# Second layer's attention on f16 high and low parts turned by transposing DMAs, with norms on ScalarE

## The chip, the cores and the metric

One core of a Trainium2 chip runs the whole kernel. The metric is the device time of one execution in microseconds (us); lower is better. TensorE (PE) multiplies and can also transpose, VectorE (DVE) and ScalarE (ACT) do elementwise work and reach PSUM, GpSimd (POOL) does elementwise work on SBUF only, and SyncE (SP) issues the DMAs. Each engine runs its own list of instructions strictly in order and meets the others at semaphores.

## The reference, cut to what matters

Two layers work on x, 32 sequences of 64 tokens of 256 numbers. The first is an eight-head cross attention and a mixture of eight experts. The second layer, where the change lies, is

```
xn   = layernorm(x)                                   # norm 3
s    = xn @ ctx^T / sqrt(256), masked keys -> -1e30   # per sequence, 64 x 64
x    = x + tanh(g_xattn[1]) * softmax(s) @ ctx
xn   = layernorm(x)                                   # norm 4
x    = x + tanh(g_ffn[1]) * FFN2(xn)                  # four experts by token position, silu(gate)*up, down
```

## The kernel before, in words

All engines run the same loop of half steps. There are 39 steps n of 8 half steps i, and h = 8n + i numbers a half step. Up to h = 255 each half step does one head of the first attention; from h = 26 on, each pair of half steps also does one unit of the feed-forward network: 24 matmuls for the gate into psG (even h), 24 for the up half into psU (odd h), tanh and the cast of the high part on ACT (`unit_tanh`, `unit_high`), two multiplications on DVE (`gate_mul`, `up_mul`), the low f16 part on POOL (`h_low`, L583), the down matmuls (`unit_down`) in the two half steps after that, and `add_expert` on DVE. In this way each f32 product is made from f16 parts, high and low. The 128 units of the first layer are followed by eight units of the second, two for each of four groups k. Their gate matmuls stand at h = 282, 284, 286, 288, 292, 294, 300 and 302. `late_y_out` (ACT), `late_y_turn` (PE) and `late_out` (DVE) bring a finished group back to token order, and `store_out` stores it.

The second attention runs in eight rounds t of four sequences each, woven into the half steps from h = 262 on. `late_base(t)` = 264 + 4t, and `late_at` gives each engine the steps r = h - late_base(t) from -2 to 7, so that two rounds are in flight. In round t:

- r = -2: DVE takes the statistics (`late_stats`, after the last `add_expert` of these tokens) and the mask (`late_masks`); POOL does the norm (`late_norm`: a power, L597, and two 128x256 subtract-and-multiply instructions, L601).
- r = 0 and 1: PE turns the normed x into psT and the context into ps1 (f32 transposes, L1007), ACT copies both (L762).
- r = 2: PE makes the scores in f32 into psV, DVE masks them (`late_masked`, L1361), ACT takes the exponentials (`late_exps`, L767).
- r = 3: PE turns them (L1100), ACT copies. r = 4: PE multiplies with the context in f32 (`late_read`), DVE adds to x (`late_attend`) and takes the statistics of norm 4; POOL does norm 4.
- r = 6 and 7: PE turns the result into psM, ACT and DVE cut it into the f16 parts of x4T.

In addition, four half steps (h = 267, 271, 275, 279) cut the second layer's weights into parts: `late_w_high` on ACT and `late_w_low` on DVE (L1335, two instructions).

The first attention's probabilities already go through transposing DMAs: `turn(g)` on SP moves a 128x1024 f16 tile, high and low part, from p_parts to p_turn (L428). SP's list is in order too: an issue waits for the semaphores of the issue ahead of it.

Of the kernel before, what the change touches and what calls it, by code (L numbers as in the profile page):

```python
# [62 lines left out]
Y_OUT_AT = [8 * TAIL_STEP + at for at in (26, 33, 37, 44)]  # L63
Y_TURN_AT = [8 * TAIL_STEP + at for at in (32, 36, 38, 45)]
# [5 lines left out]
X_SCALE = 256.0  # L70
G_UNSCALE = 1.0 / (W_SCALE * X_SCALE)
# [16 lines left out]
def build(nc, A, out):  # L88
# [14 lines left out]
    with ctx:  # L103
# [41 lines left out]
            d0_loaded d1_loaded dw_hi dw_split xt3_done ctxT_done sc_done sc_masked  # L145
            c_exp pT_ready pT_done read_done xn4T xn4_hi xn4_split cx0_loaded cx1_loaded
            d_yevac d_yT d_out xn3_ready xn4_ready xn3T cxT ln3_in ln4_in out0_stored out1_stored
# [60 lines left out]
        ctxT = lb("ctxT", [P, 2, KT, P], F32)  # L208
        x3T = lb("x3T", [P, 2, KT, P], F32)
        xn3 = lb("xn3", [P, 2, D], F32)  # L210
        d_gu = lb("d_gu", [P, 2, NE1, KT, 2 * NI1], F16)
        d_dn = lb("d_dn", [P, 2, NE1, IB1, D], F16)
        d_st = lb("d_st", [P, 2, 1536], F32)
        x4T = lb("x4T", [P, 4, 2, KT, NE1, P], F16)
        xn4 = lb("xn4", [P, 2, D], F32)
        neg = lb("neg", [P, 2, P], F32)
        pc = lb("pc", [P, 2, P], F32)
        pT = lb("pT", [P, 2, P], F32)
        cstat = lb("cstat", [P, 2, 2, 6], F32)
        cmv = lb("cmv", [P, 2, 2, 2], F32)  # L220
        cve = lb("cve", [P, 2, 2], F32)
        crs = lb("crs", [P, 2, 2], F32)
        low = lb("low", [P, 2], F32)
        csum = lb("csum", [P, 2], F32)
# [44 lines left out]
        def late_y_banks(k):  # L269


            return (psT[:, :], ps1[:, :, :].rearrange("p a b -> p (a b)")) if k % 2 == 0 else (psV[:, :], psM[:, :])
# [53 lines left out]
        def late_cut_at(n, i):  # L326


            e = (8 * (n - TAIL_STEP) + i) // 4
            return e if i % 4 == 3 and 0 <= e < NE1 else None  # L330
# [31 lines left out]
        def _(sp):  # L362
# [38 lines left out]
            def load_late_ctx(j):  # L401
                if j >= 2:
                    sp.wait_ge(s["read_done"], j - 1)
                sp.dma_start(ctx2[:, j % 2, :, :], A["ctx_2048"].rearrange("(j u b) s d -> j (b s) u d", u=2, b=2)[j]
                             ).then_inc(s[f"cx{j % 2}_loaded"], 16)

            def open_late():
# [5 lines left out]
                             ).then_inc(s["mask_m_loaded"], 16)  # L413

# [17 lines left out]
            def step(n):  # L432
                q, par = n // 2, n // 2 % 2
                even = n % 2 == 0
                for i in range(8):
# [19 lines left out]
                    for t, r in late_at(n, i):  # L455
                        if r == 5 and t + 2 < ROUNDS:
                            load_late_ctx(t + 2)
                    out_group = group_at(Y_TURN_AT, g - 1)
# [5 lines left out]
                if n == TAIL_STEP - 2:  # L464
# [3 lines left out]
                if n == TAIL_STEP - 1:  # L468
                    for e in range(2):
                        load_late_weights(e)  # L470
# [31 lines left out]
        def _(pool):  # L502
# [91 lines left out]
            def late_norm(t, kind):  # L594

                pool.wait_ge(s[f"ln{3 + kind}_in"], t + 1)
                st.link(pool.tensor_tensor(crs[:, kind, :], cve[:, kind, :], minus_half[:, 0:2], ALU.pow))  # L597
# [15 lines left out]
            def step(n):  # L613
                q, tail = n // 2, tail_pair(n)
                for i in range(8):
# [31 lines left out]
        def _(act):  # L647
# [112 lines left out]
            def late_copy(sem_in, j, dst, ps, sem_out):  # L760
                act.wait_ge(s[sem_in], j + 1)
                act.activation(dst, ps, ACT.Copy).then_inc(s[sem_out], 1)  # L762

            def late_exps(t):
                act.wait_ge(s["sc_masked"], t + 1)
                for u in range(2):
                    act.activation(pc[:, u, :], psV[:, u * P:u * P + P], ACT.Exp, bias=low[:, u:u + 1], scale=-1.0,  # L767
                                   accum_out=csum[:, u:u + 1]).then_inc(s["c_exp"], 1)

            def late_x_high(t):  # L770

                act.wait_ge(s["xn4T"], t + 1)
                for u in range(2):
                    at = t % 2 * 64 + 32 * u
                    act.activation(x4T[:, t // 2, 0, :, :, at:at + 32],
                                   psM[:, u * D:u * D + D].rearrange("p (k q e) -> p k e q", k=KT, e=NE1),
                                   ACT.Copy, scale=X_SCALE).then_inc(s["xn4_hi"], 1)

# [16 lines left out]
            def step(n):  # L795
                q, tail = n // 2, tail_pair(n)
                for i in range(8):
# [19 lines left out]
                    for t, r in late_at(n, i):  # L817
                        if r == 0:
                            late_copy("xn3T", t, x3T[:, :, :, :].rearrange("p u k t -> p (u k t)"), psT[:, :], "xt3_done")
                        elif r == 1:  # L820
                            late_copy("cxT", t, ctxT[:, :, :, :].rearrange("p u k t -> p (u k t)"),
                                      ps1[:, :, :].rearrange("p a b -> p (a b)"), "ctxT_done")
                        elif r == 2:
                            late_exps(t)
                        elif r == 3:
                            late_copy("pT_ready", t, pT[:, :, :].rearrange("p u t -> p (u t)"), ps1[:, 0, :], "pT_done")
                        elif r == 6:
                            late_x_high(t)
                    e = late_cut_at(n, i)
# [18 lines left out]
        def _(pe):  # L848
# [154 lines left out]
            def late_turn(bank, src, done):  # L1003
                for u in range(2):
                    for k in range(KT):
                        at = (u * KT + k) * P
                        last = pe.transpose(bank[:, at:at + P], src[:, u, k * P:k * P + P], ident[:, :])  # L1007
                last.then_inc(s[done], 1)

            def late_unit_in(u, bank, which, done):  # L1010
# [3 lines left out]
                for e in range(NE1):  # L1014
                    j = 0
                    for kt in range(KT):
                        for wp, xp in ((0, 0), (1, 0), (0, 1)):
                            last = mm(bank[:, e * P:e * P + P], d_gu[:, wp, e, kt, i0:i0 + P], x4T[:, k, xp, kt, e, :],
# [4 lines left out]
            def late_unit_gate(u):  # L1023
# [4 lines left out]
                if u % 2 == 0:  # L1028
                    pe.wait_ge(s["xn4_split"], 8 * (k + 1))
# [23 lines left out]
            def late_y_turn(k):  # L1053

                pe.wait_ge(s["d_yevac"], 2 * k + 2)
                if k == 0:
                    pe.wait_ge(s["xt3_done"], ROUNDS)
                    pe.wait_ge(s["pT_done"], ROUNDS)
                elif k == 1:
                    pe.wait_ge(s["x3_done"], NPAIR)  # L1060
                    pe.wait_ge(s["xn4_split"], 4 * ROUNDS)
                else:
                    pe.wait_ge(s["d_out"], 2 * (k - 1))
                for tt, bank in enumerate(late_y_banks(k)):
# [7 lines left out]
            def late_read(t, r):  # L1072
# [413 lines left out]
```

## Time and profile before

| | |
|---|---|
| median of 3 runs | 871.92 us (870.4 to 872.4) |
| the profiled execution's own time | 872.53 us |
| its span, first to last instruction | 870.8 us |
| busy in the span: PE, DVE, POOL, ACT | 779.9, 674.5, 625.2, 595.7 us |
| mean granted TensorE clock | 0.960 of full |

The span is what the trace shows; the own time is 1.73 us more. Busy times are sums over stages that differ: up to 700 us PE is busy nearly all the time, after that no engine is.

### The profile page before, as it was taken

Reading aid. Unit: us, or ns where it says so; the run is one execution under the profiler, and the core shown is the slowest. Engines: PE = TensorE matmul, PEld = TensorE weight load, DVE = VectorE, ACT = ScalarE, POOL = GpSimd, SP = SyncE. Lnnn points to the kernel's source line nnn. Section 1 sums busy time; section 2 is a strip of 40 time slices with the busy share of each in tenths; the row PEclk is TensorE's granted clock in tenths of the full one; section 3 lists DMA queues with packets and bytes.
Section 4 is the critical chain, followed back from the end, with each engine's and each line's share of the span. In section 5 each row is a group of like instructions: output and inputs, shape, how many; then the busy total and the mean of one; then the engine's idle time right before and its main releaser. Section 6 shows DMA issues by size and latency. Waiting matters only on the chain. (4 is left out here: it accounts for less than half of the span.)

```text
span 870.8 us, 30114 instructions
## 1 busy us (share of the span) xinstructions
PE 779.9 (90%) x11511; PEld 723.5 (83%) x11511; DVE 674.5 (77%) x2353; ACT 595.7 (68%) x1298; POOL 625.2 (72%) x649
## 2 busy tenths in 40 slices
PE   3466689999999999999999999999999998778876
PEld 2344489999999999999999999999999988667766
DVE  3675778888888888888888888888888865867653
ACT  3366868778787877878787778787877843434432
POOL 4265638787979797888888887979796753666651
PEclk9856789999999999999999999999999999999999
DMA  7579998879899888878899888797889662210002
GB/s 231 165 164 234 243 217 200 142 140 155 145 160 148 147 162 148 162 140 170 142 163 150 161 150 161 142 153 154 141 157 149 112 115 75 72 39 14 26 26 73
DMA packets 319541, 123.00 MB, mean 141 GB/s; under 512 B 274716, under 2 KB 312612, under 8 KB 319396
## 3 DMA queue, kind: packets, MB, share of 16 engines
q1 hardware_dynamic: 318656, 120.53, 72.1%
q8 instruction: 91, 1.49, 0.7%
q10 hardware_dynamic: 740, 0.54, 0.2%
q14 instruction: 54, 0.44, 0.2%
HBM read 45.53 MB, written 8.39 MB: 62 GB/s over the span
## 5 line engine op out<-in xcount | busy, mean ns | idle before, releaser
L591 POOL TENSOR_TENSOR p_parts<-p,p_parts 128x512 f16<-128x512 f32 x256 | 296.6, 1159 | 114.9 <-ACT p_parts L710 104.9
L583 POOL TENSOR_TENSOR hp_lo<-th_ga_h,hp_hi 128x512 f16<-128x512 f32 x136 | 157.7, 1160 | 56.1 <-ACT hp_hi L732 52.8
L850 PE MATMUL psG<-xT,w_gu 128*128 128x128 f16 x3072 | 193.5, 220 | 3.0 <-DVE th_ga_h L1286 2.6
L850 PE MATMUL psU<-xT,w_gu 128*128 128x128 f16 x3072 | 194.0, 220 | 0.1
L850 PE MATMUL psY<-w_dn,hp_hi 128*128 128x256 f16 x1024 | 182.2, 273 | 4.5 <-POOL hp_lo L583 4.5
L850 PEld LDWEIGHTS psG<-xT,w_gu 128*128 128x128 f16 x3072 | 176.3, 98 | 7.4 <-DVE th_ga_h L1286 4.9
L850 PEld LDWEIGHTS psU<-xT,w_gu 128*128 128x128 f16 x3072 | 177.7, 98 | 1.0 <-DVE th_ga_h L1294 0.2
L710 ACT ACTIVATE p_parts<-p 128x512 f16<-128x512 f32 x256 | 160.6, 627 | 6.8 <-DMA p_turn<-p_parts 6.3
L1210 DVE CUSTOM_DVE_ANT_0 ps<-ps,mask_in 128x256 f32<-128x256 f32 x256 | 104.2, 448 | 55.3 <-PE ps L850 54.3
L850 PE MATMUL psY<-w_dn,hp_lo 128*128 128x256 f16 x512 | 139.9, 273 | 0.0
L702 ACT ACTIVATE p<-ps,exp_bias 128x256 f32<-128x256 f32 x256 | 107.1, 469 | 47.1 <-DVE exp_bias L1214 46.1
L702 ACT ACTIVATE p<-psT,exp_bias 128x256 f32<-128x256 f32 x256 | 107.3, 473 | 40.2 <-DVE exp_bias L1214 32.7
L726 ACT ACTIVATE th_ga_h<-psG 128x512 f32<-128x512 f32 x136 | 81.2, 597 | 67.8 <-PE psG L850 66.2
L1210 DVE CUSTOM_DVE_ANT_0 psT<-psT,mask_in 128x256 f32<-128x256 f32 x256 | 103.6, 446 | 14.9 <-PE psT L850 14.9
L850 PEld LDWEIGHTS psV<-v_parts,p_turn 128*128 128x128 f16 x2048 | 88.9, 97 | 31.2 <-DMA p_turn<-p_parts 24.7
L850 PEld LDWEIGHTS psY<-w_dn,hp_hi 128*128 128x128 f16 x1024 | 98.3, 98 | 18.8 <-POOL hp_lo L583 6.4
L850 PE MATMUL psV<-v_parts,p_turn 128*128 128x25 bf16 x2048 | 91.4, 175 | 18.7 <-DMA p_turn<-p_parts 16.5
L1286 DVE SCALAR_TENSOR_TENSOR th_ga_h<-th_ga_h,psG 128x512 f32<-128x512 f32 x136 | 93.4, 687 | 12.1 <-ACT th_ga_h L726 11.4
L1294 DVE SCALAR_TENSOR_TENSOR th_ga_h<-psU,th_ga_h 128x512 f32<-128x512 f32 x136 | 92.0, 676 | 4.9 <-PE psU L850 3.7
L732 ACT ACTIVATE hp_hi<-th_ga_h 128x512 f16<-128x512 f32 x136 | 85.8, 631 | 2.0 <-DVE th_ga_h L1294 2.0
L1210 DVE DVE_READ_ACCUMULATOR2_ANT low_max<- 128x1 f32 x512 | 72.6, 142 | 0.0
L1304 DVE SCALAR_TENSOR_TENSOR x_res<-psY,tokw,x_res 128x256 f32<-128x256 f32 x128 | 60.8, 475 | 2.7 <-PE psY L850 2.6
(180 smaller groups left out, 1077.5 us busy)
## 6 DMA issues: line engine op xcount, KB each, us to landing
mask_in<-in_mask_Bx2048x_ff SPq DMA_DIRECT2D x32, 256.0 KB, 3.1
part_scratch<-parts SPq DMA_DIRECT2D x16, 384.0 KB, 3.8
q_stack<-part_scratch SPq DMA_DIRECT2D x62, 96.0 KB
k_stack<-part_scratch SPq DMA_DIRECT2D x62, 96.0 KB
stage<-in_L_ffn_gate_w SPq DMA_DIRECT2D x8, 512.0 KB, 4.9
stage<-in_L_ffn_up_w SPq DMA_DIRECT2D x8, 512.0 KB, 4.9
stage<-in_L_ffn_down_w SPq DMA_DIRECT2D x8, 512.0 KB, 4.3
p_turn<-p_parts SPq DMA_TRANSPOSE x256, 3.6
```

What stands on the lines that cost most here:

```text
L583: pool.tensor_tensor(hp_lo[:, u % 2, :], hb32[:, u % 2, :], hp_hi[:, u % 2, :], ALU.subtract).then_inc(s["h_split"], 1)
L591: pool.tensor_tensor(p_parts[:, g % 4, 1, :, :], p32[:, g % 2, :, :], p_parts[:, g % 4, 0, :, :], ALU.subtract).then_inc(s["plo_done"], 1)
L702: act.activation(p32[:, g % 2, nt, :], score_bank(g)[:, nt, :], ACT.Exp, bias=exp_bias[:, g % 2, nt:nt + 1], scale=-1.0).then_inc(s["exp_d ...
L710: act.activation(p_parts[:, g % 4, 0, :, :], p32[:, g % 2, :, :], ACT.Copy).then_inc(s["phi_done"], 1)
L726: act.activation(th, psG[:, :], ACT.Tanh, scale=0.5 * G_UNSCALE).then_inc(s["tanh_done"], 1)
L732: act.activation(hp_hi[:, u % 2, :], hb32[:, u % 2, :], ACT.Copy).then_inc(s["h_hi"], 1)
L850: return pe.matmul(out_, lhsT, rhs, start=start, stop=stop, skip_group_check=shares_bank)
L1210: dve.tensor_tensor_reduce(out=score_bank(g)[:, nt, :], in0=score_bank(g)[:, nt, :], in1=mask_in[:, n % 2, nt, :], scale=-1.0, scalar=HIGH ...
L1286: dve.scalar_tensor_tensor(out=ga, in0=th, scalar=1.0, in1=psG[:, :], op0=ALU.add, op1=ALU.mult).then_inc(s["gate_used"], 1)
L1294: dve.scalar_tensor_tensor(out=hb32[:, u % 2, :], in0=psU[:, :], scalar=0.5 * G_UNSCALE * G_UNSCALE, in1=ga, op0=ALU.mult, op1=ALU.mult).t ...
L1304: dve.scalar_tensor_tensor(out=x_res[:, row, :], in0=psY[:, y_bank(u), 0:D], scalar=tokw[:, row * NE + e:row * NE + e + 1], in1=x_res[:, r ...
```

## The change

The second attention gets the same treatment as the first: operands are cut into high and low f16 parts on ACT and POOL, turned by DMA, and multiplied in three f16 matmuls where there was one of f32. The f32 transposes on PE and the copies out of PSUM go.

- A round has r = -2 to 10 and `late_base(t)` = 260 + 4t, so that three rounds are in flight and round 0 starts four half steps earlier.
- The norm is done on ACT (`late_norm`, two 128x256 instructions and a 128x512 cast to the high part). POOL keeps the power, one small multiplication (`late_pow`), and takes the low parts (`late_low`, `late_ctx_low`, `late_p_low`).
- SP issues four transposing DMAs a round: the normed x and the context at r = 1, the exponentials at r = 5, norm 4's output at r = 10.
- The scores stand at r = 3 in ps1, the second product at r = 7, `late_attend` and the statistics of norm 4 at r = 8.
- Output groups are turned in psT and psM only, at other half steps; the weights' loads and cuts move by one or two half steps.

In the diff below, "..." marks what is left out: semaphore names, buffer declarations (cx_parts has three buffers, cxT, x3T and pc_parts one), and lines that only rename.

```diff
-Y_OUT_AT = [8 * TAIL_STEP + at for at in (26, 33, 37, 44)]
-Y_TURN_AT = [8 * TAIL_STEP + at for at in (32, 36, 38, 45)]
+Y_OUT_AT = [8 * TAIL_STEP + at for at in (26, 30, 36, 44)]
+Y_TURN_AT = [8 * TAIL_STEP + at for at in (27, 31, 37, 45)]
...
-            return 8 * TAIL_STEP + 4 * t
+            return 8 * TAIL_STEP - 4 + 4 * t
...
-            return [(t, r) for t, r in at if -2 <= r <= 7]
+            return [(t, r) for t, r in at if -2 <= r <= 10]
...
+            def turn_xn3(t):
+                sp.wait_ge(s["xn3_lo"], t + 1)
+                if t:
+                    sp.wait_ge(s["sc_done"], t)
+                turn_late(x3T[:, :, :, :, :].rearrange("p a u k t -> p (a u k) t"),
+                          xn3_parts[:, :, :, :].rearrange("p a u d -> p (a u d)"), "xn3_turned")
+
+            def turn_ctx(t):
+                sp.wait_ge(s["cx_lo"], t + 1)
...
+            def turn_pc(t):
+                sp.wait_ge(s["pl_lo"], t + 1)
+                if t:
+                    sp.wait_ge(s["read_done"], t)
...
+            def turn_xn4(t):
+                sp.wait_ge(s["xn4_lo"], t + 1)
...
                     for t, r in late_at(n, i):
-                        if r == 5 and t + 2 < ROUNDS:
+                        if r == 0 and t + 2 < ROUNDS:
                             load_late_ctx(t + 2)
+                        elif r == 1:
+                            turn_xn3(t)
+                            turn_ctx(t)
+                        elif r == 5:
+                            turn_pc(t)
+                        elif r == 10:
+                            turn_xn4(t)
...
+            def late_pow(t, kind):
...
                 st.link(pool.tensor_tensor(crs[:, kind, :], cve[:, kind, :], minus_half[:, 0:2], ALU.pow))
-                if t:
-                    pool.wait_ge(s[f"xn{3 + kind}T"], t)
-                for u in range(2):
-                    pool.tensor_scalar((xn3, xn4)[kind][:, u, :], x_res[:, 2 * t + u, :], cmv[:, kind, u, 0:1],
-                                       crs[:, kind, u:u + 1], ALU.subtract, ALU.mult).then_inc(s[f"xn{3 + kind}_ready"], 1)
+                pool.tensor_tensor(csh[:, kind, :], cnm[:, kind, :], crs[:, kind, :], ALU.mult
+                                   ).then_inc(s[f"pow{3 + kind}_done"], 1)
+
+            def late_low(t, kind):
+
+                pool.wait_ge(s[f"xn{3 + kind}_hi"], t + 1)
+                parts_of, full = (xn3_parts, xn4_parts)[kind], (xn3, xn4)[kind]
+                pool.tensor_tensor(parts_of[:, 1, :, :], full[:, :, :], parts_of[:, 0, :, :], ALU.subtract
+                                   ).then_inc(s[f"xn{3 + kind}_lo"], 1)
...
                     for t, r in late_at(n, i):
-                        if r == 4:
-                            late_norm(t, 1)
                         if r == -2:
-                            late_norm(t, 0)
+                            late_pow(t, 0)
+                        elif r == -1:
+                            late_ctx_low(t)
+                        elif r == 0:
+                            late_low(t, 0)
+                        elif r == 5:
+                            late_p_low(t)
+                        elif r == 8:
+                            late_pow(t, 1)
+                        elif r == 10:
+                            late_low(t, 1)
...
+            def late_norm(t, kind):
+                act.wait_ge(s[f"pow{3 + kind}_done"], t + 1)
+                if t:
+                    act.wait_ge(s[f"xn{3 + kind}_lo"], t)
+                    act.wait_ge(s[f"xn{3 + kind}_turned"], 16 * t)
...
+                    act.activation(full[:, u, :], x_res[:, 2 * t + u, :], ACT.Identity,
+                                   scale=crs[:, kind, u:u + 1], bias=csh[:, kind, u:u + 1]
...
-                        if r == 0:
-                            late_copy("xn3T", ...
...
+                        if r == -2:
+                            late_ctx_high(t)
+                        elif r == -1:
+                            late_norm(t, 0)
+                        elif r == 4:
                             late_exps(t)
...
+                        elif r == 9:
+                            late_norm(t, 1)
...
+            def late_scores(t):
+
+                pe.wait_ge(s["xn3_turned"], 16 * (t + 1))
+                pe.wait_ge(s["cx_turned"], 16 * (t + 1))
...
+                    for k in range(KT):
+                        for xp, cp in ((0, 0), (1, 0), (0, 1)):
+                            last = mm(ps1[:, 0, u * P:u * P + P], x3T[:, xp, u, k, :], cxT[:, cp, u, k, :],
...
+            def late_read(t):
+
+                pe.wait_ge(s["pl_turned"], 16 * (t + 1))
...
-                        late_read(t, r)
+                        if r == 3:
+                            late_scores(t)
+                        elif r == 7:
+                            late_read(t)
...
+                st.link(dve.tensor_scalar(cnm[:, kind, :], cmv[:, kind, :, 0], -1.0, None, ALU.mult))
...
-                last.then_inc(s["sc_masked"], 1)
+                    st.link(dve.tensor_tensor_reduce(out=at, in0=at, in1=neg[:, u, :], scale=-D ** -0.5 / (X_SCALE * C_SCALE),
...
+                dve.tensor_scalar(low_bias[:, t % 2, :], low[:, t % 2, :], LOG_P_SCALE, None, ALU.add
+                                  ).then_inc(s["sc_masked"], 1)
...
                         if r == -2:
                             late_stats(t, 0)
+                        elif r == 1:
                             late_masks(t)
-                        elif r == 2:
+                        elif r == 3:
                             late_masked(t)
-                        elif r == 4:
+                        elif r == 8:
                             late_attend(t)
                             late_stats(t, 1)
-                        elif r == 7:
-                            late_x_low(t)
```

## Rows read from the trace of the kernel before

**Rows 1.** Busy time by round: stretch, length, five engines, granted clock, DMA share, GB/s

```profile
core 0: us, PE busy (x) PEld busy (x) DVE busy (x) ACT busy (x) POOL busy (x), PEclk, DMA share, GB/s
722.81:738.70 15.89, 13.61 (x164) 12.37 (x162) 7.10 (x21) 5.51 (x14) 6.32 (x7) 0.89 0.06 21
...
767.30:782.90 15.60, 12.12 (x149) 10.61 (x147) 11.52 (x32) 6.74 (x15) 10.24 (x9) 1.00 0.06 18
...
798.49:811.54 13.05, 12.08 (x148) 10.71 (x147) 9.15 (x30) 5.29 (x13) 8.65 (x9) 1.00 0.08 23
...
837.91:852.15 14.24, 9.53 (x101) 8.34 (x99) 7.89 (x26) 4.81 (x13) 5.43 (x5) 0.91 0.11 38
852.15:870.80 18.65, 11.77 (x170) 10.99 (x168) 6.26 (x10) 4.88 (x8) 2.31 (x2) 0.96 0.26 86
```

**Rows 2.** Waits after 700 us: who waited for whom, total us, times, longest

```profile
POOL crs L597 <- DVE cve L1346: 43.3, 16, 5.6
...
PEld psM L1007 <- POOL xn L601: 11.2, 8, 2.8
```

**Rows 3.** Timeline of a round: start, us, engine, line, operation, count [idle before <-releaser]

```profile
811.05 0.66 PE L1007 MATMUL psM<-ident,xn 128*128 128x128 f32 x4 [0.25 <-POOL xn L601]
...
811.54 1.06 PE L850 MATMUL psV<-ctxT,x3T 128*128 128x128 f32 x8
...
820.79 0.72 POOL L597 TENSOR_TENSOR crs<-cve,minus_half 128x2 f32<-128x2 f32 x1 [1.61 <-DVE cve L1346]
...
821.62 2.43 POOL L601 TENSOR_SCALAR xn<-x_res,cmv,crs 128x256 f32<-128x256 f32 x2
```

**Rows 4.** Timeline, VectorE's work around the masking and the second product

```profile
803.34 0.68 DVE L1294 SCALAR_TENSOR_TENSOR th_ga_h<-psU,th_ga_h 128x512 f32<-128x512 f32 x1
...
805.23 0.88 DVE L1374 SCALAR_TENSOR_TENSOR x_res<-psV,cr,x_res 128x256 f32<-128x256 f32 x2 [0.29 <-PE psV L850]
...
806.14 0.89 DVE L1343 BATCH_NORM_STATS2 cstat<-x_res 128x6 f32<-128x256 f32 x2
...
807.50 0.17 DVE L1346 TENSOR_SCALAR cve<-cmv 128x2 f32<-128x2 f32 x1
...
812.64 0.30 DVE L1361 CUSTOM_DVE_ANT_0 psV<-psV,neg 128x128 f32<-128x128 f32 x1 [2.65 <-PE psV L850]
...
812.85 0.14 DVE L1361 DVE_READ_ACCUMULATOR2_ANT low<- 128x1 f32 x1
```

**Rows 5.** Groups and single instructions on POOL: subtractions and small multiplications

```profile
L583 POOL TENSOR_TENSOR hp_lo<-th_ga_h,hp_hi 128x512 f16<-128x512 f32 x136 | 157.7, 1160 | 56.1 <-ACT hp_hi L732 52.8
...
58.33 0.22 POOL L571 TENSOR_TENSOR shift<-mean_var,rstd 128x14 f32<-128x14 f32 x1
...
59.99 0.69 POOL L528 TENSOR_TENSOR rem<-rem,v_parts 128x256 f32<-128x256 f32 x1
...
72.88 0.41 POOL L609 TENSOR_TENSOR on<-o_sum,o_rec 128x128 f32<-128x128 f32 x1 [1.50 <-DMA p_turn<-p_parts]
```

**Rows 6.** SP: instructions on p_turn and on d_st, ns min/median/max, and landing

```profile
L428 SPq DMA_TRANSPOSE p_turn<-p_parts x256: 1231/1267/2821, 42.0 to 710.7; - x128
...
DMA to landing us min/median/max: 3.0/3.6/7.8
...
L417 SPq DMA_DIRECT2D out<-d_st x8: 372/372/1085, 845.7 to 868.0; - x8
...
L1395 DVE TENSOR_TENSOR d_st<-psT,x_res x2: 683/683/683, 845.0 to 858.9; 128x512 f32<-128x512 f32 x2
```

**Rows 7.** Timeline, the cut of one expert's low weight parts on VectorE

```profile
772.56 1.23 DVE L1335 SCALAR_TENSOR_TENSOR d_gu<-d_st,d_gu 128x1024 f16<-128x1024 f32 x1 [0.34 <-ACT d_dn L783]
...
773.70 0.68 DVE L1335 SCALAR_TENSOR_TENSOR d_dn<-d_st,d_dn 128x512 f16<-128x512 f32 x1
```

**Rows 8.** Timeline, an up half of a unit on PE at h = 263

```profile
723.23 1.50 PE L850 MATMUL psU<-xT,w_gu 128*128 128x128 f16 x24
```

**Rows 9.** Group of the first layer's second norm on ScalarE: total us, mean ns

```profile
L747 ACT ACTIVATE xn<-x_res,shift,rstd 128x256 f32<-128x256 f32 x16 | 9.6, 600 | 11.7 <-POOL shift L578 11.6
```

More of the change, by code:

```diff
@@ L70 @@
 X_SCALE = 256.0
+C_SCALE = 16.0
 G_UNSCALE = 1.0 / (W_SCALE * X_SCALE)
@@ L207, in build @@
         m_u8 = lb("m_u8", [P, NPAIR, P], U8)
-        ctxT = lb("ctxT", [P, 2, KT, P], F32)
-        x3T = lb("x3T", [P, 2, KT, P], F32)
+        cx_parts = lb("cx_parts", [P, 3, 2, 2, D], F16)
+        cxT = lb("cxT", [P, 2, 2, KT, P], F16)
+        x3T = lb("x3T", [P, 2, 2, KT, P], F16)
         xn3 = lb("xn3", [P, 2, D], F32)
+        xn3_parts = lb("xn3_parts", [P, 2, 2, D], F16)
+        neg = lb("neg", [P, 2, P], F32)
+        xn4 = lb("xn4", [P, 2, D], F32)
+        xn4_parts = lb("xn4_parts", [P, 2, 2, D], F16)
+        pc = lb("pc", [P, 2, P], F32)
+        pc_parts = lb("pc_parts", [P, 2, 2, P], F16)
+        pT = lb("pT", [P, 2, 2, P], F16)
         d_gu = lb("d_gu", [P, 2, NE1, KT, 2 * NI1], F16)
@@ L324, in late_weight, with late_cut_at @@
                     (d_st[:, e % 2, 1024:1536].rearrange("p (t i) -> p t i", t=IB1), d_dn[:, part, e, :, :]))
-        def late_cut_at(n, i):
+        def late_cut_at(n, i, cut):
             e = (8 * (n - TAIL_STEP) + i) // 4
-            return e if i % 4 == 3 and 0 <= e < NE1 else None
+            return e if i % 4 == cut and 0 <= e < NE1 else None
         def load_stacks(eng, par, q, piece):
@@ L764, in late_exps @@
             def late_exps(t):
                 act.wait_ge(s["sc_masked"], t + 1)
+                if t:
+                    act.wait_ge(s["pl_lo"], t)
+                    act.wait_ge(s["pl_turned"], 16 * t)
                 for u in range(2):
[L767 to L777, printed above, removed]
+                    act.activation(pc[:, u, :], ps1[:, 0, u * P:u * P + P], ACT.Exp, bias=low_bias[:, t % 2, u:u + 1],
+                                   scale=-1.0, accum_out=csum[:, t % 2, u:u + 1]).then_inc(s["c_exp"], 1)
@@ L779, in late_w_high @@
+                act.wait_ge(s["c_exp"], 2 * t + 2)
+                act.activation(pc_parts[:, 0, :, :], pc[:, :, :], ACT.Copy).then_inc(s["pl_hi"], 1)
             def late_w_high(e):
@@ new lines, in late_scores @@
+            def late_scores(t):
+                pe.wait_ge(s["xn3_turned"], 16 * (t + 1))
+                pe.wait_ge(s["cx_turned"], 16 * (t + 1))
+                if t == 0:
+                    pe.wait_ge(s["exp_done"], 2 * 8 * B)
+                else:
+                    pe.wait_ge(s["c_exp"], 2 * t)
+                for u in range(2):
+                    j = 0
+                    for k in range(KT):
+                        for xp, cp in ((0, 0), (1, 0), (0, 1)):
+                            last = mm(ps1[:, 0, u * P:u * P + P], x3T[:, xp, u, k, :], cxT[:, cp, u, k, :],
+                                      start=(j == 0), stop=(j == 5))
+                            j += 1
+                last.then_inc(s["sc_done"], 1)
@@ new lines, in late_read @@
+            def late_read(t):
+                pe.wait_ge(s["pl_turned"], 16 * (t + 1))
+                if t == 0:
+                    pe.wait_ge(s["pv_evac"], B)
+                else:
+                    pe.wait_ge(s["x3_done"], 2 * t)
+                for u in range(2):
+                    for j, (pp, cp) in enumerate(((0, 0), (1, 0), (0, 1))):
+                        last = mm(psV[:, u * D:u * D + D], pT[:, pp, u, :], cx_parts[:, t % 3, cp, u, :],
+                                  start=(j == 0), stop=(j == 2))
+                last.then_inc(s["read_done"], 1)
@@ L1310, in _ @@
             st.link(dve.tensor_scalar(bias_v[:, :], bias_v[:, :], gates[:, 0:1], None, ALU.mult))
+            st.link(dve.tensor_scalar(gates[:, 1:2], gates[:, 1:2], 1.0 / C_SCALE, None, ALU.mult))
             dve.wait_ge(s["qk_copied"], 2)
```

177 lines of the change are left out of this document (72 added, 105 removed).

## The prediction

> **What bounds the kernel now.** Read the page first: its slices show PE busy all through the first attention and the feed-forward units, and only from about 700 us on no engine full. The change touches that last part alone, so everything below is about it. Next, the busy times by round of the second attention [rows 1]: the stretches are cut where the scores of successive rounds start. A round takes 15.6 us while the second layer's weights are cut and 13.05 us later, and in 13.05 us PE is busy 12.1, DVE 9.2, POOL 8.7 and ACT 5.3: nobody is full, so a chain through several engines sets the round. The waits say which [rows 2]: POOL waits 43.3 us, 16 times, for the variance that DVE hands it before each norm, and PE waits for POOL's normed x. One round shows the same in order of time [rows 3]: the power starts at 820.79, the normed x is there at 821.62 + 2.43 = 824.05, and PE, which met the previous norm in the same way at 811.05, goes on to the scores. Two such norms of 0.83 + 2.43 us lie in every round, with DVE's statistics ahead and a PE turn behind.
>
> **What goes.** On POOL 2 x 2.43 us a round. On PE twelve f32 transposes of x and context (0.66 for four [rows 3]), two of exponentials, f32 scores of 1.06 us and a second product of about as much; 24 f16 matmuls of 128 columns take 1.50 us [rows 8], so the twelve of the new scores 0.75, and the six of 256 columns of the new second product the same. PE's 12.1 us fall to about 9. ACT loses four copies and gains nine instructions a round that I bound by 0.60 each [rows 9]: at most 5.3 + 5.4 = 10.7 us. None of the engines' sums fills a round of 13 us. So the next question is which chain closes on itself.
>
> **The chain that I find.** Four half steps hold parts of three rounds. Put S at the end of the scores of round t-1, and go on in the order of the lists.
>
> 1. DVE: `late_masked` of t-1. An instruction starts 0.21 before its accumulator read, which takes 0.14 [rows 4]; with a link behind each now, 0.43 twice, then the new small addition 0.17. S + 1.07.
> 2. DVE: `up_mul`, `add_expert`, `late_attend` of t-2. From 803.34 to 806.14 these take 2.80 us, of which 0.29 waiting [rows 4]. S + 3.58.
> 3. DVE: statistics of norm 4 of t-2, 806.14 to 807.67, plus one more linked small instruction, 0.21. S + 5.35.
> 4. POOL: the power, 0.83 to the next start [rows 3], and the small multiplication, 0.22 [rows 5], with 0.1 of hand-over: S + 6.5. Then, queued behind it, `late_low` of t (1.16), `h_low` of the unit (1.16), `late_p_low` of t-1. This last is 128x256: between 0.41 (half as large) and 1.16 (twice as large), and I take 0.69, the row of that size [rows 5]. S + 9.5.
> 5. SP, which has waited for that low part: `turn_pc` of t-1, and only behind it `turn_xn3` and `turn_ctx` of t. A transposing DMA of 128x1024 holds SP for at least 1.23 us and lands 3.0 at best and 3.6 in the median after its issue [rows 6]. `turn_pc` has half the size: between 0.37, a plain store, and 1.23; I take 0.9, since a transposing issue is the nearer row. The context is issued at S + 9.5 + 0.9 + 1.23 = S + 11.65 and lands, at 3.3, at S + 14.95.
> 6. PE: scores of t, 0.75 and 0.1 of start. S + 15.8.
>
> The scores of t are what DVE masks next, so a round takes 15.8 us. With the shortest values (0.41 for the low part, 0.37 and 3.0) it is 14.7, with the longest (1.16 for the low part, 1.23, 3.6) 16.9. The four rounds in which `late_w_low` follows the masking get 1.14 + 0.6 = 1.74 us more, from start to start [rows 7]: 17.5. PE, ACT and the norms of t+1 lie beside the chain: PE's 9 us of work end about 5 us before the round does, and this slack hides their new instructions. If the chain were shorter, the next thing late would be the unit's own loop, below. The context's low part is ready a round ahead; only SP's order makes it late. The same order decides for x, because `turn_xn3` stands behind `turn_pc` too. The moved DMAs cost nothing on SP: the first two experts' weights wait for the last product of the first attention, which precedes them by two half steps, and the early stores wait for an addition that is done 5 us before the `turn_pc` behind them.
>
> **The sum.** The clock starts in a half step that both kernels have. At h = 263 PE starts an up half at 723.23 [rows 8]; the first scores end about 723.23 + 1.5 + 0.85 = 725.6 (round 0's earlier steps lie under the first attention). The first interval has no `late_attend`, statistics or power in it: masking 1.1, exponentials and cast 1.3 (three instructions, none larger than 0.60), the unit's cast 0.6, `h_low` 1.16, `late_p_low` 0.69, SP and DMA 5.4, scores 0.85: 11.1. Then four of 17.5 and two of 15.8: the last scores end at 725.6 + 11.1 + 70 + 31.6 = 838.3. Before, they started at 837.91 and took 1.06 [rows 1, 3]. So the four half steps' head start is used up by then.
>
> What follows has grown. Before, 13.2 us lie from there to the gate matmuls of the last group at 852.15 [rows 1]. Now, in us after the last scores: output group 0 is turned and added (eight f32 transposes 1.2, two additions of 0.68 [rows 6], less overlap) 2.6; `late_attend` and statistics of round 6 5.9; power 7.0; `late_p_low` 7.7; `turn_pc` landed 10.9; second product 11.6; group 1 turned and added 14.0; `late_attend` of round 7 15.6; statistics 17.3; power 18.4; norm on ACT (three instructions of about 0.6) 20.2; low part 21.4; `turn_xn4` landed 24.6. The gate starts at 838.3 + 24.6 = 862.9, and the end comes 18.65 us later, as before [rows 1]: 881.5.
>
> The profiled execution's own time is 872.53, 1.73 above its span, so 883.3; the median of the runs stands 0.6 below the profiled one, so **882.6 us**, 1.2% slower.
>
> **A rule that speaks against the rows.** A transposing issue here takes 1.23 us of SP, three times the 0.37 of a plain store, and lands in 3.0 to 3.6 [rows 6]. The Trainium skill (Advanced Engine Details and Errata, X-Bar Transpose (TRN2)) says that transposing DMAs on this chip are as fast as regular ones. By the rows the chain costs 15.8 a round, by that rule step 5 would shrink as in the second rival; the trace does not agree for the issue.
>
> **Rivals.**
>
> - *The turns are hidden, faster.* If the three turns landed by the time that PE has reached the scores anyway, the unit's loop would set the round: DVE's list from the masking to `gate_mul` (5.3 + 0.6), gate and down 2.2, up 1.5, second product and scores 1.5, with hops about 11.4, with the weights' cut 13.1. Then the last scores end at 725.6 + 11.1 + 52.4 + 22.8 = 811.9, the span at 855, the time at 856. It decides if the context lands 4 us earlier. For it: low DMA share in this part [rows 1]. Against it: the order on POOL and SP, and 3.0 us is the fastest of 256 landings [rows 6].
> - *Turns cheaper than the rows, no change.* With issues of 0.37 and landings of 2.6, the round falls to 9.5 + 0.74 + 2.6 + 0.85 = 13.7 and the six full intervals lose 2.1 each: 870 to 876. For it: all 256 turns were timed beside other traffic. Against it: their 1.23 us minimum is flat.
> - *The clock falls, slower still.* PE's granted clock was 0.89 and 0.91 in two stretches where it waited [rows 1], though it stayed 1.00 in the rounds. PE would now be idle over a third of a round. At the half level (1.2 GHz) a round's 9 us become 18, PE becomes the bound, and six rounds of 18 in place of four of 17.5 and two of 15.8 with a slow last group give about 892. The Trainium skill (TensorE: Matmul & The Clock Gate, Part 1) says that idle gaps bring the clock to half; the two stretches agree.
>
> **Chances.** The chain as found 0.58; clock 0.15; turns cheaper 0.14; turns hidden 0.13. The chain's own range is 14.7 to 16.9 a round, which is 7 us either way around 882.6, and 2 us more for the start. The range reaches down into the cheap turns and up to the falling clock: 869 to 893. This kernel can tell 0.2%, 1.7 us. Faster takes the hidden turns and a little of the cheap ones: 0.16; the same 0.06; slower 0.78.
>
> **What would show it.** In the profile after: scores about 16 to 17.5 us apart; PE's longest waits ahead of the scores, released by the DMA into cxT or x3T; SP's three turns back to back, starting right after POOL's low part of the exponentials; POOL's `late_pow` idle for DVE, then four instructions without a gap; 24 us from the last scores to the last group's gate. The prediction is wrong if the context's turn is landed before PE asks, if SP's issues are far below 1.23 us, or if rounds are under 14 us.

## The result, and the profile after

The changed kernel takes 899.17 us in the median of four runs (898.74 to 899.63), the kernel before 872.16 beside it: a ratio of 1.031, 95% interval 1.030 to 1.033. It is slower, as forecast, but by 27 us where 10.7 were forecast, and 899 lies above the range of 869 to 893. The profiled execution has a span of 897.0 (870.8 before).

First the stretches between the starts of successive scores, and the two stretches of the tail; columns as in [rows 1].

```profile
726.99:740.17 13.18, 9.96 (x144) 9.19 (x145) 7.78 (x22) 9.39 (x21) 8.84 (x11) 1.00 0.67 188
740.17:758.17 18.00, 11.76 (x138) 10.18 (x139) 14.90 (x42) 9.18 (x21) 6.83 (x9) 0.91 0.44 104
776.18:794.48 18.30, 12.84 (x139) 10.70 (x139) 11.93 (x31) 9.40 (x20) 8.00 (x10) 0.83 0.32 65
812.19:828.94 16.75, 15.61 (x145) 14.89 (x146) 9.38 (x29) 8.07 (x18) 8.02 (x10) 0.90 0.39 56
828.94:844.52 15.58, 10.70 (x114) 9.67 (x115) 6.04 (x20) 6.50 (x15) 5.97 (x7) 0.87 0.32 59
844.52:874.04 29.52, 21.78 (x214) 21.25 (x215) 11.94 (x35) 9.43 (x19) 6.98 (x9) 0.85 0.26 63
874.04:897.00 22.96, 16.12 (x160) 15.51 (x160) 5.34 (x8) 3.61 (x6) 2.31 (x2) 0.87 0.14 46
```

A round of 15.6 to 18.3 us stands where 13.05 and 15.6 stood, and in most of them no engine is full. The last row is the surprise: the last stretch has 170 matmuls before and 160 after, but PE is busy 16.1 us in it instead of 11.8.

The waits after 700 us say who closes the loop (columns as in [rows 2]):

```profile
POOL crs L644 <- DVE cve L1413: 75.8, 13, 11.4
...
DVE ps L1429 <- PE ps L931: 38.1, 8, 8.5
...
PEld ps L931 <- issue: 15.3, 6, 2.9
```

POOL now waits 75.8 us for DVE's variance (43.3 in [rows 2]), DVE waits for the scores, and the scores wait too (the row of PEld; "issue" means that the profile names no releaser). The chain of waits through one round (start, us, what; only the larger pieces) puts these in order:

```profile
776.18 1.45 PE ps L931 x12
...
778.52 0.12 DVE d_gu L1399
...
780.35 0.60 DVE th_ga_h L1357
...
782.82 0.44 DVE cstat L1409
...
784.63 0.71 POOL crs L644
...
785.60 1.11 POOL xn_parts L652
786.71 0.73 POOL hp_lo L628
...
787.77 0.68 POOL pc_parts L662
788.48 1.20 SPq L425
...
789.77 3.25 DMA x3T<-xn_parts
793.02 1.46 issue
794.48 0.84 PE ps L931 x12
```

This is the forecast loop, step by step: masking, low weight parts, `up_mul`, attend, statistics, power, three low parts, three turns on SP (`turn_pc` at 788.48, `turn_xn3` at 789.77, `turn_ctx` right behind at 791.07), scores. The last 1.46 us, "issue" to the profile, fit the landing of the context's turn, for which `late_scores` waits: the scores start 3.41 us after its issue, and the turns into cxT land in 3.1 to 4.1.

What the forecast did not have stands in the timeline of the tail:

```profile
860.51 0.84 PE L931 MATMUL psV<-cx_parts,pT 128*128 128x256 f16 x6
...
874.04 2.94 PE L931 MATMUL psG<-x4T,d_gu 128*128 128x128 f16 x24 [2.34 <-DMA x4T<-xn_parts]
876.81 2.96 PE L931 MATMUL psU<-x4T,d_gu 128*128 128x128 f16 x24
...
883.25 2.96 PE L931 MATMUL psU<-x4T,d_gu 128*128 128x128 f16 x24
```

24 f16 matmuls of 128 columns took 1.50 us in [rows 8]. Here the late units' take 2.94 to 2.97, all sixteen of these groups. The change has an edit at just this place, which the diff shown before the prediction leaves out (cut to what matters):

```diff
 # late_unit_in, the moving operand
-                x4T[:, k, xp, kt, e, :],
+                x4T[:, k % 2, :, xp, :, kt, :].rearrange("p t u (q e) -> p e t u q", e=NE1)[:, e],
```

The turn leaves x4T in token order, so that `late_unit_in` reads every fourth token of it, a step of four f16 elements. Besides, a DMA writes x4T now, where ACT and DVE did.

### The profile page after: what moved, and what is told of

Read it like the earlier page. It is cut to its first block and busy times, and to the rows that moved or that the text cites. A ratio compares the mean times of both kernels' runs of the same rounds, so it can differ in the third digit from the quotient of the medians.

```text
span 897.0 us, 30108 instructions
## 1 busy us (share of the span) xinstructions
PE 791.1 (88%) x11447; PEld 736.5 (82%) x11447; DVE 677.4 (76%) x2346; ACT 616.4 (69%) x1330; POOL 614.6 (69%) x665
## 5 line engine op out<-in xcount | busy, mean ns | idle before, releaser
L931 PE MATMUL psG<-xT,w_gu 128*128 128x128 f16 x3072 | 196.3, 221 | 7.0 <-DVE th_ga_h L1349 6.6
L931 PEld LDWEIGHTS psG<-xT,w_gu 128*128 128x128 f16 x3072 | 179.4, 99 | 10.7 <-DVE th_ga_h L1349 8.1
L931 PE MATMUL psY<-w_dn,hp_hi 128*128 128x256 f16 x1024 | 184.4, 275 | 4.1 <-POOL hp_lo L628 4.0
L644 POOL TENSOR_TENSOR crs<-cve,minus_half 128x2 f32<-128x2 f32 x16 | 11.2, 698 | 76.1 <-DVE cve L1413 75.8
```

The source lines that it names most:

```text
L931: return pe.matmul(out_, lhsT, rhs, start=start, stop=stop, skip_group_check=shares_bank)
```

## The experiments

The theory after this first look: the loop through POOL's and SP's order sets the rounds as forecast, and the strided read of x4T is the cost that was not forecast. The rivals: the clock slowed those matmuls (PE's granted clock does fall, to 0.83 to 0.91 in the rounds); the transposing DMAs are themselves the limit, whatever the order.

**1. Adjacent tokens in x4T, all else as changed.**

```diff
- x4T[:, k % 2, :, xp, :, kt, :].rearrange("p t u (q e) -> p e t u q", e=NE1)[:, e]
+ x4T[:, k % 2, :, xp, :, kt, 32 * e:32 * e + 32]
```

> The changed kernel, but the late units' gate and up products read 32 adjacent tokens of each block per expert instead of every fourth token. Each expert so gets other tokens: this part of the output is changed. Theory (the read with a step of four f16 elements is what makes 24 matmuls of 128 columns take 2.94 us instead of 1.50): the groups return to about 1.5 us at the same granted clock, the last group's gate comes 3.5 us sooner after the last scores, the end 4.3 us sooner after that gate, and the rounds stay at 15.6 to 18 us because another chain sets them: 890 to 893 us. Rival (the clock made these groups slow): they stay at 2.9 us and the time stays at 899. Rival (PE's longer late units also set the rounds): rounds shorten by up to 2.9 us each, 875 to 885.

890.94 us (889.9 to 894.0), 8.2 less than the changed kernel. Timeline and windows of its tail:

```profile
869.64 2.72 PE L931 MATMUL psG<-x4T,d_gu 128*128 128x128 f16 x24 [2.32 <-DMA x4T<-xn_parts]
...
874.82 1.50 PE L931 MATMUL psG<-x4T,d_gu 128*128 128x128 f16 x24
```

```profile
843.95:869.64 25.69, 17.52 (x214) 16.59 (x215) 11.94 (x35) 9.22 (x19) 7.00 (x9) 0.77 0.30 73
869.64:888.50 18.86, 12.14 (x160) 11.38 (x160) 5.34 (x8) 3.61 (x6) 2.31 (x2) 0.86 0.17 56
...
869.64:872.15 2.51, 2.51 (x24) 2.51 (x25) 0.00 (x0) 0.00 (x0) 0.00 (x0) 0.50 0.00 0
```

From the end of the last scores (843.95 + 1.44) to the last group's gate are 24.25 us, forecast 24.6; from there to the end 18.86, forecast 18.65. So the strided read is what made the tail longer than forecast, by 7.9 us, and the rounds with weights stayed (18.1, 18.3, 17.7, 17.8). The first row needs care: 2.72 us looks like the strided 2.94, but there the granted clock was 0.50, the 1.2 GHz level. A strided read is told from a slow clock only with the granted clock beside it.

**2. The kernel before, with the strided read alone** (x4T kept in token order by the two casts; `late_unit_in` as in the changed kernel).

```diff
- x4T = lb("x4T", [P, 4, 2, KT, NE1, P], F16)
+ x4T = lb("x4T", [P, 4, 2, KT, 2, 2, P], F16)
- act.activation(x4T[:, t // 2, 0, :, :, at:at + 32], ...
+ act.activation(x4T[:, t // 2, 0, :, t % 2, u, :], ...
- ... x4T[:, k, xp, kt, e, :],
+ ... x4T[:, k, xp, kt, :, :, :].rearrange("p t u (q e) -> p e t u q", e=NE1)[:, e],
```

> The kernel before, with one part of the change alone: its turned x is kept in token order (the casts to high and low part write it so), and the late units read every fourth token of it. Theory: each of the sixteen groups of 24 matmuls takes 2.9 us instead of 1.50. The last four halves alone cost 4.3 to 5.8 us. In a round of 13.05 us PE is busy 12.1, and two groups more by 1.45 each make it 15.0, so up to 2 us a round for six rounds come on top: 877 to 890, likeliest 884. Rival (the clock, or the transposing DMA that writes x, made them slow): 24 matmuls stay at 1.50 us, and the time at 872.

889.73 us, ratio to the kernel before 1.019 (1.015 to 1.024), at the upper end of what was expected. The group of these matmuls, columns as in [rows 5]:

```profile
L849 PE MATMUL psG<-x4T,d_gu 128*128 128x128 f16 x192 | 23.6, 294 | 0.8 <-DVE x4T L1384 0.8
```

192 matmuls in 23.6 us are 2.95 us for 24 (successive matmuls overlap, so the 294 ns of a single one don't add up), and no transposing DMA writes x4T here. In the old loop PE had little to spare: the three rounds with late units took 17.05, 15.49 and 16.91 us instead of 13.05, 13.05 and 13.32, and the read cost about 17 us in all (the 1.9% of the ratio). In the changed kernel's loop, where PE waits, it cost only 8.

**3. Which step costs.** Groups 0 to 3 read with a step of 1, 2, 3 and 4.

```diff
+ x4T[:, k % 2, :, xp, :, kt, 0:32 * (k + 1):k + 1]
```

> The changed kernel, whose late units read the turned x with a step of 1, 2, 3 and 4 elements in the groups 0, 1, 2 and 3 (32 tokens of each block, the same for all four experts: this part of the output is changed). Theory (one full-rate read for adjacent elements, one slow rate for any step): 24 matmuls take 1.50 us in group 0 and 2.94 in the three others. Rival (the cost grows with the distance): 1.50, then about 2.0, 2.5 and 2.94; or full rate up to a step of two and 2.94 beyond. In all cases the time lies a little below the changed kernel's, 894 to 898.

897.86 us, inside what was expected. Timeline, one `psU` group at each step, all four at a granted clock of 1.00:

```profile
805.09 1.50 PE L931 MATMUL psU<-x4T,d_gu 128*128 128x128 f16 x24
...
821.75 1.52 PE L931 MATMUL psU<-x4T,d_gu 128*128 128x128 f16 x24
...
856.56 2.30 PE L931 MATMUL psU<-x4T,d_gu 128*128 128x128 f16 x24
...
881.42 2.96 PE L931 MATMUL psU<-x4T,d_gu 128*128 128x128 f16 x24
```

None of the three patterns that were named: a step of two is free, three costs half as much again, four twice. The Trainium skill (Advanced Engine Details and Errata, SBUF Cachelines) says that SBUF has lines of 16 bytes and that it takes at least two hits on a line to absorb the latency of a read. A step of four f16 elements has two hits on each line, and the runs here show half speed all the same, so the measurement decides: two hits weren't enough for this read.

**4. The order of SP and PE**: the newer round first inside a half step.

```diff
 # in SP's and PE's lists
-                    for t, r in late_at(n, i):
+                    for t, r in reversed(late_at(n, i)):
```

> The changed kernel with the order of two queues turned round inside a half step: SP issues the turns of x and context of round t ahead of the turn of the exponentials of round t-1, and PE does the scores of t ahead of the second product of t-1. Theory (a loop through POOL's and SP's order sets the round): the context's turn is issued when POOL's low part of x is done, 786.7 instead of 791.1 in the round that starts at 776.2, so its scores come about 3.4 us sooner. Rounds of 12.4 us in place of 15.6, of 14.5 in place of 18, and the last scores 15 to 22 us sooner: 877 to 886. Rival (the turns' own duration or the units' work sets the round, whatever the order): rounds within 1 us of 18 and 15.6, 897 to 901.

882.01 us (879.9 to 884.0), 17 less, inside what was expected: the order of the two lists, and not the turns' length by itself, made the rounds long. (Which of the two lists counts was not tried apart.) But the rounds were 16.8, 16.7, 14.9, 15.4, 15.1 and 12.5, not 14.5 and 12.4, and part of the gain came from the first interval, 9.58 instead of 13.18. One of the windows shows what came next:

```profile
799.00:814.10 15.10, 15.10 (x147) 14.79 (x145) 9.08 (x29) 7.48 (x17) 7.47 (x10) 1.00 0.51 71
```

PE is full, at the full clock, with four strided groups: once the queue's order is out of the way, the strided read is on the path of the rounds too.

**5. POOL's order**: the power of norm 4 a half step later, behind the low part of the exponentials.

```diff
 # in POOL's list
-                    for t, r in late_at(n, i):
+                    for t, r in sorted(late_at(n, i), key=lambda at: at[1] == 9):
...
-                        elif r == 8:
+                        elif r == 9:
                             late_pow(t, 1)
```

> The changed kernel with POOL's order alone changed: the power of norm 4 of round t-2 stands behind the low part of the exponentials of t-1, a half step later, instead of ahead of the low part of x of round t. Theory (the loop goes from the masking through DVE's statistics to the power, and the low parts are late because they stand behind it): with the power out of the way the low part of the exponentials follows the exponentials and the unit's low part, about 4 us sooner, and SP's three turns with it. Rounds of 11.5 to 13.5 us late, 13.5 to 15 with the weights' cut, 873 to 885. Rival (the loop isn't through the power): rounds as they were or longer, 898 to 903.

889.55 us, 9.6 less: the power is on the loop, but the gain is half of what was expected. (The profiled execution, 886.56, is the fastest of the four, and its first attention ended 3.5 us sooner than the changed kernel's; from the first scores to the last it took 110.2 us instead of 117.5.) Rounds of 14.6 to 18.1 remain. The timeline of one shows DVE's low weight parts and POOL's subtraction of the context:

```profile
754.50 1.21 DVE L1399 SCALAR_TENSOR_TENSOR d_gu<-d_st,d_gu 128x1024 f16<-128x1024 f32 x1
754.52 2.20 POOL L657 TENSOR_TENSOR cx_parts<-ctx,cx_parts 128x512 f16<-128x512 f32 x1
...
755.64 1.64 DVE L1399 SCALAR_TENSOR_TENSOR d_dn<-d_st,d_dn 128x512 f16<-128x512 f32 x1
```

Alone POOL's takes 1.16 and DVE's second 0.68 [rows 5, 7]; here POOL's lasts 1.04 longer, beside DVE's first, and DVE's second 0.96 longer, beside POOL's. The times fit the three taking turns: DVE to 755.71, POOL to 756.72, DVE to 757.28. How much of the missing gain this makes is not shown. The Trainium skill (SBUF — State Buffer, Who interferes with whom) says that a DVE instruction with two SBUF inputs and a POOL instruction that reads SBUF contend for a shared port, which one instruction holds at a time; these rows agree.

**6. Both orders**, with the strided and with the adjacent read.

> The changed kernel with both reorderings (SP and PE by the newer round first; the power of norm 4 a half step later on POOL). Each alone gave 882.0 and 889.6 us. Theory (once the queues' order is out of the way, what is left is the units' work: DVE's list with the weights' low parts, 15 to 16.7 us a round as the chain of the run with POOL's order alone shows, then PE with late units of 2.94 us a half, 15.1 us a round): the two together gain little over the better one, 876 to 883, with the late rounds still at 15. Rival (the queues' order still sets the rounds in each of the two): together they add up, 870 to 875.

> Both reorderings, and the late units read 32 adjacent tokens per expert instead of every fourth (each expert gets other tokens, so this part of the output is changed). Theory (with the queues' order out of the way PE's late units of 2.94 us set the late rounds, and the tail has the same four halves): late rounds of 12 to 13.5 us instead of 15, three of them, and 7 to 8 us less in the tail: 13 to 16 us less than with both reorderings alone, 862 to 868. Rival (the strided read costs only where it did with the old order, 8 us): 870 to 873.

883.67 us strided: the second reordering adds nothing to the first, a little above what was expected. 872.35 us adjacent (ratio to before 1.001, 0.998 to 1.003): 11.3 less, where the same edit was worth 8.2 in the old order. Expected were 862 to 868: the last two rounds came out as forecast, at 13.3 and 12.5, but the four with weights still took 15.2 to 16.6.

**7. The low weight parts ahead of the masking**, in the changed kernel alone (`late_w_low` before the loop over `late_at` in DVE's list).

> The changed kernel with one DVE step moved: the low parts of the second layer's weights stand ahead of the masking of the scores in the half steps that have both, not behind it. Theory (in four rounds the weights' low parts lie on the loop with 1.74 us each, between the masking and the units' products; ahead of the masking DVE waits anyway, up to 8 us a round): the four rounds of 17.7 to 18.3 us become 16 to 16.5, the time 890 to 893. Rival (the weights' low parts are long because POOL works beside them, and what comes first on the loop is PE or POOL): no change, 897 to 901.

893.75 us, 5.4 less and a little above what was expected; the four rounds took 16.6 to 16.8 instead of 17.7 to 18.3. That confirms the term of 1.74 us a round, of which about 1.3 was gained (72.02 − 66.71, by four).

**8. The first interval**: the context's low part a half step earlier on POOL.

> The changed kernel with one POOL step moved a half step ahead: the low part of the context of a round stands right behind the power of norm 3, not beside DVE's masking. Theory (the first interval of 13.2 us, forecast 11.1, is long because DVE's small addition takes 1.18 us beside POOL's subtraction of the context, then the exponentials and the low parts are late): that addition returns to about 0.2 us and the first interval to 12.0 to 12.4; rounds as they were; 898 in all. Rival (the addition is long for another reason): interval 13.2 and the addition at 1.2.

A miss: 901.27 us, first interval 14.05. The step did not leave the masking's side, since POOL came to it only after a wait of 4.33 us for the power's input:

```profile
730.12 1.16 POOL L657 TENSOR_TENSOR cx_parts<-ctx,cx_parts 128x512 f16<-128x512 f32 x1
...
730.70 0.61 DVE L1431 TENSOR_SCALAR low_bias<-low 128x2 f32<-128x2 f32 x1
```

The addition ends here with POOL's instruction, at 731.31 against 731.28. It did so in the changed kernel too, at 729.82 against 729.80:

```profile
728.64 1.16 POOL L657 TENSOR_TENSOR cx_parts<-ctx,cx_parts 128x512 f16<-128x512 f32 x1
728.64 1.18 DVE L1432 TENSOR_SCALAR low_bias<-low 128x2 f32<-128x2 f32 x1
...
729.85 0.60 ACT L795 ACTIVATE th_ga_h<-psG 128x512 f32<-128x512 f32 x1 [0.86 <-PE psG L931]
730.34 0.36 ACT L858 ACTIVATE pc<-ps,low_bias 128x128 f32<-128x128 f32 x1
```

So the neighbour does stretch the addition. But that is not what makes the interval long: the exponentials (730.34) stand in ACT's order behind the unit's tanh, which waits for its gate matmuls on PE. They start 3.35 or 3.36 us after the start of the scores in the changed kernel and in experiments 7, 5 and 1 alike, whose additions take 1.18, 0.47, 0.63 and 0.90, and the first interval is 13.2 in all four. In this run they start 4.12 us after it: POOL's part of another norm, for which ACT waits ahead of the tanh, now comes behind the moved subtraction.

**9. A version that is not slower.** Both orders, and two ACT copies a round from token order into a tile sorted by expert; then with the low weight parts first; then with the last round's steps earlier.

```diff
+ act.activation(x4E[:, t // 2 % 2, :, :, :, at:at + 32].rearrange("p a k e q -> p (a k) e q"),
+                x4T[:, t % 2, u, :, :, :].rearrange("p a k (q e) -> p (a k) e q", e=NE1), ACT.Copy)
...
-    x4T[:, k % 2, :, xp, :, kt, :].rearrange("p t u (q e) -> p e t u q", e=NE1)[:, e]
+    x4E[:, k % 2, xp, kt, e, :]
```

> Both reorderings, and x4T sorted by expert again: after the turn of the normed x, two ACT instructions of a round copy it from token order to a second tile in which each expert's tokens are adjacent, and the late units read that one as before the change. Theory: groups of 24 matmuls at 1.50 us; the copies cost ACT about 1.2 us a round, hidden in the rounds, and lie once on the path to the last group's gate: 2 us more than the run with adjacent tokens, 864 to 870, faster than the kernel before. Rival (ACT's wait for the turn holds up the units' tanh, or the copy's own step of four elements is as slow there): 872 to 880.

> Both reorderings and the sorted copy (873.0 us, as fast as the kernel before), with the weights' low parts ahead of the masking too. Theory (there DVE's list is the loop in the four rounds with weights, so what it is freed of comes off the round): rounds of 13 to 14 us in place of 15 to 16, 863 to 867, faster than the kernel before by 0.6 to 1%. Rival (PE and the clock set these rounds): 871 to 874.

> As the run before this one, and the last round's steps after its scores lie one to two half steps earlier in every list, so that its second product stands ahead of the late unit that it waited for (834.7 instead of 840.8), with the last group's units and output two half steps earlier. Theory (in the tail the last round's chain waits in PE's order and nothing else is late): 4 to 6 us less than without it, 858 to 863. Rival (the late unit, now behind, is itself on the path through the output groups): no gain.

872.98 us (1.002, 1.000 to 1.005), 870.66 (0.998, 0.997 to 1.000) and 869.63 (0.997, 0.995 to 0.999). All three fell short of what was expected: the first lies in the range of its rival, and the rounds with weights of the second took 13.7 to 15.9 instead of 13 to 14. The last one beats the kernel before by 0.3%, but its 1.0 us over the second is within the spread of its runs (865.5 to 873.4), so it comes close to its rival's "no gain". From the last scores to the end it took 45.6 us, the second 47.4. Why the tail gained so little stands in its timeline:

```profile
825.90 0.17 DVE L1450 TENSOR_SCALAR low_bias<-low 128x2 f32<-128x2 f32 x1
...
827.61 1.23 ACT L874 ACTIVATE x4E<-x4T 128x512 f16<-128x512 f16 x2 [4.30 <-DMA x4T<-xn_parts]
...
830.52 0.60 ACT L800 ACTIVATE th_ga_h<-psG 128x512 f32<-128x512 f32 x1 [1.68 <-PE psG L949]
831.01 0.36 ACT L863 ACTIVATE pc<-ps,low_bias 128x128 f32<-128x128 f32 x1
```

The last round's exponentials could start at 826.1, but stand in ACT's order behind the copy, which waits for a turn, and a tanh, which waits for the unit: 5 us. The rival of the sorted copy's expectation, ACT held up by its wait for the turn, so has a part in it. An order without that was not tried.

## Why the prediction was wrong

The profiled spans, 897.0 against 881.5 forecast, differ by 15.5 us; the rest of the 16.6 between the medians is that the profiled execution lay 0.4 below the median, not 0.7 above it. Term by term, from the starts of the scores (the terms are rounded):

| term | forecast | measured | difference |
|---|---|---|---|
| first scores end | 725.6 | 727.82 | +2.2 |
| first interval | 11.1 | 13.18 | +2.1 |
| four rounds with weights | 70.0 | 72.02 | +2.0 |
| two rounds without | 31.6 | 32.33 | +0.7 |
| last scores, longer than the first ones' 0.83 | 0 | 0.61 | +0.6 |
| last scores to the last gate | 24.6 | 28.08 | +3.5 |
| last gate to the end | 18.65 | 22.96 | +4.3 |

**What bounds the rounds: right.** The loop named in six steps is the one in the chain of waits, and its sizes hold within 0.4 us each. From the end of the scores at 777.62 (776.18 + 1.44): masking 0.90 (forecast 1.07), low weight parts 1.74 (1.74), to the statistics 2.56 (2.51), statistics 1.74 (1.77), POOL's steps 3.9 (4.15), turns of SP 1.29 and 1.30 (0.9 and 1.23), landing 3.41 (3.3), scores 0.84. Experiments 4, 5 and 7 each took one of these out of the way, and the time fell.

**The step that failed: "and the end comes 18.65 us later, as before".** The late units' matmuls were carried over at their old price, 24 in 1.50 us. But the diff turns x4T by a DMA and so leaves it in token order, and its `late_unit_in` takes every fourth element; that part of the diff got no price at all. Experiment 1 gives its size in the tail, 3.8 + 4.1 us (28.08 − 24.25 and 22.96 − 18.86), and without it both tail terms come out within 0.4 us of the forecast. The first of the two is PE's order: `turn_pc` of the last round, issued at 853.78, lands 2.5 us later, but the second product starts only at 860.51, behind four halves of 2.95, 14.55 us after the last scores. In experiment 1 it waits for the landing instead and starts after 10.74.

**Mis-sized terms of the loop, +7.6 together.** `turn_pc` was taken at 0.9 us because it is half as large; it holds SP 1.20, nearly as long as the whole ones:

```profile
L425 SPq DMA_TRANSPOSE x3T<-xn_parts x8: 1242/1250/2282, 721.4 to 839.8; - x8
...
L425 SPq DMA_TRANSPOSE pT<-pc_parts x8: 1190/1196/1202, 734.3 to 853.8; - x8
```

That is 0.3 in each of seven intervals, some 2 us. The start was taken as hidden under the first attention; but the first turn of x held SP 2.28 us (the longest of the eight), the context's turn was issued at 723.76, and PE waited 1.16 us for its landing. In experiment 1 that turn held SP 1.24, and PE waited 0.33: part of this is chance. The rest of the start's 2.2 is that the first attention ended 1.1 us later in this execution: its last product started at 717.91 against 716.82, and between 714.4 and 720.8 in the profiles of all the runs. Of the first interval's 2.1, 1.4 is a wait on ACT that the sum left out: it put the exponentials right behind the masking, 1.1 us after the scores, but they stand behind the unit's tanh and start 2.5 after (experiment 8). Another 0.4 is in the turns.

**The rivals.** Turns hidden, or cheaper than the rows: no; in the median they land in 2.5 to 3.3 us and hold SP 1.20 to 1.34. The falling clock: it fell, to 0.83 to 0.91 in the rounds, and costs what the last scores show, 1.44 instead of 0.83, but it explains neither the tail (experiment 1 has a lower clock there, 0.77 against 0.85, and is faster) nor the rounds: of the chain PE holds only the scores, and a round with weights took 17.75 us at a granted clock of 1.00 in experiment 1 and 17.71 at 0.90 in the changed kernel. Its forecast of 892 came nearer than the chain's for another reason. (The stretch with 0.89 in [rows 1], which this rival leaned on, is not cut at the scores: it starts at 722.81, and the first scores of the kernel before start at 736.15.)

## What to carry to other kernels

When a change moves data to another producer, price the readers too: a layout that is free for the producer may be read with a step, and the same matmuls then take twice the time. With lists in order on each engine, a chain is shortened by looking at what each late step stands behind, and reordering can be worth more than speeding up any of them (17 us here); but expect the next bound at once. A cost is worth what the path leaves of it: the strided read was worth 17, 8 and 11 us in three orders of the same work.

## What the runs showed of the hardware

- A moving operand in f16 with a step of 1, 2, 3 and 4 elements: 24 matmuls in 1.50, 1.52, 2.30 and 2.96 us at a granted clock of 1.00. In the changed kernel the step of four takes 2.94 at a granted clock of 0.50 (874.04) and 2.96 at 1.00 (883.25), while adjacent elements take 2.72 and 1.50 in experiment 1: the strided read does not follow PE's clock.

```profile
874.04:877.00 2.96, 2.96 (x26) 2.96 (x27) 0.00 (x0) 0.00 (x0) 0.00 (x0) 0.50 0.02 6
...
883.00:886.00 3.00, 3.00 (x28) 2.99 (x27) 0.69 (x1) 1.12 (x2) 1.16 (x1) 1.00 0.30 99
```

- A transposing DMA of half the size holds SP 1.20 us against 1.25, and lands in 2.5 against 3.2.
- DVE's subtraction of 128x512 (0.68 alone) took 1.64 beside POOL's, and POOL's (1.16 alone) 2.20. Even a DVE addition of 128x2 (0.17 alone) that met a POOL subtraction lasted until its end: 1.18 us in the changed kernel, 0.61 in experiment 8.
